# The rows of the MLP turned by VectorE and a scratch in device memory instead of by TensorE

## What is computed

```python
h = _ln(win, ln1_g, ln1_b)
q, k, v = h @ wq + bq, h @ wk + bk, h @ wv + bv
attn = softmax(q k^T / sqrt(32));  o = attn @ v
win = win + (o @ wo + bo)
h2 = _ln(win, ln2_g, ln2_b)
win = win + gelu(h2 @ w1 + b1) @ w2 + b2        # w1: 96 x 384, w2: 384 x 96
```

## Time and profile before

| | |
|---|---|
| median of 3 runs | 5434.65 us (5433.81 to 5440.99) |
| the profiled execution | 5443.81 us, span 5442.0 us |
| PE busy | 5176.5 us, 95% of the span |
| DVE / ACT / POOL busy | 77% / 69% / 57% |
| DMA queue of SyncE | 208 MB, 13.0% of 16 engines' span |

### The profile page before, as it was taken

One profiled execution on the slowest core, in us unless ns is written; L12 is line 12 of the kernel. 1 busy time (PEld: TensorE's weight loads), 2 busy tenths in 40 slices (PEclk: granted clock), 3 DMA queues, 4 the chain that ended last, 5 costly groups with the idle time before them and its releaser, 6 DMA issues.

```text
span 5442.0 us, 275140 instructions
## 1 busy us (share of the span) xinstructions
PE 5176.5 (95%) x105172; PEld 4395.4 (81%) x105172; DVE 4179.8 (77%) x9862; ACT 3741.6 (69%) x7758; POOL 3083.7 (57%) x3053
## 2 busy tenths in 40 slices
PE   6999999999999999999999999999999999999999
PEld 4887888878788787888878888788887888878888
DVE  6968768687686877869778697786977869688696
ACT  6839568495784957749477594875938659396693
POOL 5645646466464655646556466464664646556464
PEclk8999999999999999999999999999999999999999
DMA  3011020110201102010120201202011020110201
GB/s 98 3 44 48 27 68 6 47 42 27 68 9 51 36 30 65 11 57 27 33 62 15 61 19 36 59 16 66 13 38 57 19 70 6 41 54 22 73 3 44
DMA packets 92300, 213.96 MB, mean 39 GB/s; under 512 B 22058, under 2 KB 26379, under 8 KB 91851
## 3 DMA queue, kind: packets, MB, share of 16 engines
q1 hardware_dynamic: 91848, 208.20, 13.0%
q10 hardware_dynamic: 2, 0.00, 0.0%
HBM read 107.45 MB, written 100.66 MB: 38 GB/s over the span
## 4 chain that ended last, share of the span: by engine, by line
PE 88%; issue 5%; DVE 5%; SPq 1%; ACT 1%; POOL 0%; DVEq 0%; ACTq 0%; DMA 0%; POOLq 0%
PE psum L585 20%; PE psum L599 19%; PE psum L462 12%; PE psum L430 8%; PE psum L508 6%; PE psum L477 6%; PE psum L494 6%; PE psum L538 5%; PE psum L524 5%; DVE row_max L828 1%; DVE stats L807 1%; DVE stream L857 1%; SPq L251 1%; DVE probs L835 0%; DVE prob_sum L843 0%
## 5 line engine op out<-in xcount | busy, mean ns | idle before, releaser
L297 POOL TENSOR_TENSOR probs<-probs,prob_inv 128x512 f32<-128x512 f32 x771 | 783.1, 1044 | 1496.7 <-DVE prob_inv L851 1496.6
L857 DVE TENSOR_TENSOR stream<-stream,psum 128x384 f32 x1024 | 562.4, 553 | 850.3 <-PE psum L599 760.8
L736 ACT ACTIVATE gelu_odd<-psum 128x512 f32<-128x512 f32 x768 | 459.9, 599 | 732.7 <-PE psum L585 676.9
L736 ACT ACTIVATE gelu_even<-psum 128x512 f32<-128x512 f32 x768 | 459.6, 598 | 682.8 <-PE psum L585 627.1
L376 POOL TENSOR_TENSOR stream<-stream,b_all 128x768 f32 x256 | 493.2, 1931 | 612.4 <-DVE normed L877 584.8
L659 ACT ACTIVATE normed<-stream,shift,rstd 128x96 f32 (+1 forms) x2072 | 770.7, 461 | 43.9 <-POOL shift L345 23.2
L807 DVE BATCH_NORM_STATS2 stats<-stream (+2 forms) x4224 | 725.9, 243 | 57.1 <-DVE stream L857 38.9
L336 POOL TENSOR_TENSOR rstd<-variance,minus_half 128x32 f32<-128x32 f32 (+3 forms) x181 | 747.7, 4131 | 14.2
L304 POOL TENSOR_TENSOR hT<-hT_upper,hT_lower 96x1024 f32<-96x1024 f32 x258 | 613.6, 2378 | 22.8 <-issue 15.6
L828 DVE TENSOR_REDUCE row_max<-psum 128x8 f32<-128x512 f32 x771 | 523.8, 679 | 131.7 <-PE psum L494 116.6
L843 DVE TENSOR_REDUCE prob_sum<-probs 128x8 f32<-128x512 f32 x771 | 497.8, 679 | 109.1 <-ACT probs L693 109.1
(11 more groups left out here) (86 smaller groups left out, 10635.3 us busy)
## 6 DMA issues: line engine op xcount, KB each, us to landing
stream<-in_x SPq DMA_DIRECT2D x272, 192.0 KB
out<-stream SPq DMA_DIRECT2D x256, 192.0 KB
stream<-in_x SPq DMA_DIRECT2D x272, 180.0 KB
out<-stream SPq DMA_DIRECT2D x256, 180.0 KB
stream<-in_x SPq DMA_DIRECT2D x544, 6.0 KB
out<-stream SPq DMA_DIRECT2D x512, 6.0 KB
gelu_odd<-in_L_conv_w SPq DMA_DIRECT2D x1, 144.0 KB
w_w<-in_L_conv_w SPq DMA_DIRECT2D x1, 144.0 KB
```

The lines of the kernel that those rows point to most:

```text
L297: nc.gpsimd.tensor_tensor(block_h, block_h, inv, ALU.mult).then_inc(probs_ready, 1)
L736: nc.scalar.activation(gelu[parity][:, j, part * SHARES:(part + 1) * SHARES], psum[:, UP_BANKS[part][j], :], ACT.Gelu).then_inc(gelu_done, 1)
L857: nc.vector.tensor_tensor(part, part, psum[:, banks[g], 0:GROUP], ALU.add).then_inc(added, 1)
```

## The change

The 8 transposes of each MLP unit leave TensorE. VectorE turns the normalised rows in blocks of 32x32 (`turn_h2`), which puts 32 channels of a tile on the 32 partitions of each block. SyncE sends the turned rows to a scratch in device memory with 3 DMAs, one for each block of 32 channels (`send_turned`), waits until they are there, and fetches them back as 96 partitions by 1,024 numbers with one DMA (`fetch_turned`). The scratch has 4 places; the fetched units alternate between two buffers, those of `probsT` and `oT` in the MLP stage. ScalarE makes the upper half (`copy_h2T_upper`, two copies of 96x512), VectorE the first half of the lower, GpSimd the second. Tokens arrive in another order, which `gelus` puts right by the pattern it writes with.

Units 0, 1 and 2 of a batch are normalised by GpSimd, turned by VectorE and sent during the attention stage; units 0 and 1 are also fetched there, and GpSimd makes both their halves at steps 11 and 13. `down` now waits for both parts of the Gelu and comes in one piece. The diff, cut:

```diff
+        turned_dram = nc.dram_tensor("turned_rows", (RING, CBLOCKS, BLOCK, TBLOCKS, RUN), FP32, kind="Internal").ap()
+        turned_early = gelu[1][:, 2, 0:SEG]
+        turned_late = flat_tile(normed1[:, :, :])
+        raw_early = [gelu[0][0:C, 0, :], gelu[0][0:C, 1, :]]
+        raw_late = [probsT[0:C, :, :, :].rearrange("c h q k -> c (h q k)")[:, 0:TOK], oT[0:C, :]]
...
+            def send_turned(u, source, place):
+                wait_apart(sp, h2_turned, u + 1)
+                for cb in range(CBLOCKS):
+                    sp.dma_start(turned_dram[place, cb].rearrange("c t x -> t c x"),
+                                 source[:, RUN * cb:RUN * (cb + 1)]).then_inc(h2_left, 16)
+            def fetch_turned(u, raw, place):
+                wait_apart(sp, h2_left, 16 * CBLOCKS * (u + 1))
+                sp.dma_start(raw, turned_dram[place].rearrange("b c t x -> (b c) (t x)"))\
+                    .then_inc(h2_back[place % 2], 16)
+            def fetch_late(u, place):
+                for ready in h2T_ready:
+                    wait_apart(sp, ready, u - 1)
+                fetch_turned(u, raw_late[place % 2], place)
             def store_batch(batch_row):
-                with sp.Fori(0, BATCH_ROWS) as r:
+                batch = 2 * batch_row
+                for n in range(2):
+                    send_turned(batch + n, turned_early, n)
+                    fetch_turned(batch + n, raw_early[n], n)
+                send_turned(batch + 2, turned_early, 2)
+                wait_apart(sp, pv_done, batch + BATCH)
+                fetch_turned(batch + 2, raw_late[0], 2)
+                send_turned(batch + 3, turned_late, 3)
+                fetch_late(batch + 3, 3)
+                with sp.Fori(0, 3) as q:
+                    for n in range(RING):
+                        store(batch_row + 2 * q + n // 2, n % 2)
+                        send_turned(batch + 4 * q + n + 4, turned_late, n)
+                        fetch_late(batch + 4 * q + n + 4, n)
+                for row in (6, 7):
                     for half in (0, 1):
-                        store(batch_row + r, half)
+                        store(batch_row + row, half)
...
+            def copy_h2T_early(u, parity):
+                wait_apart(pool, h2_back[parity], 8 * (u - parity) + 16)
+                whole, upper, lower = raw_early[parity], h2T[parity][0][0:C, :], h2T[parity][1][0:C, :]
+                nc.gpsimd.tensor_copy(upper, whole).then_inc(h2T_upper_early, 1)
+                return whole, upper, lower
+            def lower_early(b, u, parity, parts):
+                whole, upper, lower = parts
+                pool.wait_ge(h2T_upper_early, 2 * b + parity + 1)
+                nc.gpsimd.tensor_tensor(lower, whole, upper, ALU.subtract).then_inc(h2T_ready[0], 1)
+                pool.sem_inc(h2T_ready[1], 1)
+            def copy_h2T_lower(b, j, u, parity):
+                second = slice(SHARES, 2 * SHARES)
+                wait_apart(pool, h2T_upper_done, 2 * (BATCH - 2) * b + 2 * (j - 2) + 2)
+                nc.gpsimd.tensor_tensor(h2T[parity][1][0:C, second], raw_late[parity][:, second],
+                                        h2T[parity][0][0:C, second], ALU.subtract).then_inc(h2T_ready[1], 1)
...
                     if s == 3:
                         finish2(call, batch, 0, 2)
+                    if s == 4:
+                        normalise2(b, batch, 0)
                     if s == 5:
-                        finish2(call + 1, batch + 2, 2, 2)
+                        finish1(call + 1, batch + BATCH, 0, 2)
+                    if s == 6:
+                        normalise2(b, batch + 1, 1)
                     if s == 7:
-                        normalise2(b)
+                        finish1(call + 2, batch + BATCH + 2, 2, 1)
+                    if s == 8:
+                        finish2(call + 3, batch + 2, 2, 2)
+                    if s == 9:
+                        normalise2(b, batch + 2, 2)
                     if s == 10:
-                        finish1(call + 2, batch + BATCH, 0, 2)
+                        finish2(call + 4, batch + 4, 4, 2)
+                    if s == 11:
+                        lower_early(b, batch, 0, copy_h2T_early(batch, 0))
                     if s == 12:
-                        finish1(call + 3, batch + BATCH + 2, 2, 1)
+                        finish2(call + 5, batch + 6, 6, 2)
+                    if s == 13:
+                        lower_early(b, batch + 1, 1, copy_h2T_early(batch + 1, 1))
                     normalise_probs(batch + s + 1, (s + 1) % 2)
                 for j in range(BATCH):
+                    if j < BATCH - 2:
+                        copy_h2T_lower(b, j + 2, batch + j + 2, j % 2)
...
-            def transpose2(u, steady):
-                pe.wait_ge(ln2_ready, u + 1)
+            def up(u, parity, part, steady):
+                pe.wait_ge(h2T_ready[part], u + 1)
                 if steady:
-                    pe.wait_ge(gelu_done, 2 * FCHUNKS * u - FCHUNKS)
-                for g in range(2):
-                    transpose_rows(normed2, T2_BANKS, g, t2_done)
-            def up(u, parity, part, steady):
-                pe.wait_ge(h2T_copied, 2 * u + 1 + part)
-                if part and steady:
-                    pe.wait_ge(gelu_done, 2 * FCHUNKS * u)
+                    wait_apart(pe, gelu_done, 2 * FCHUNKS * u - FCHUNKS * (1 - part))
...
+            def mlp_step(u, parity):
+                up(u, parity, 1, True)
+                up(u + 1, 1 - parity, 0, True)
+                down(u, parity, True)
...
+                    in_rows = gelu[parity][:, j, :].rearrange("p (t b i) -> p b t i", b=TBLOCKS, i=BLOCK)
+                    nc.scalar.activation(
+                        in_rows[:, 2 * part:2 * part + 2, :, :],
+                        psum[:, UP_BANKS[part][j], :].rearrange("p (b t i) -> p b t i", b=2, i=BLOCK),
+                        ACT.Gelu).then_inc(gelu_done, 1)
+            def copy_h2T_upper(u, parity):
+                act.wait_ge(h2_back[parity], 8 * (u - parity) + 16)
+                for g in range(2):
+                    tokens = slice(g * SHARES, (g + 1) * SHARES)
+                    nc.scalar.activation(h2T[parity][0][0:C, tokens], raw_late[parity][:, tokens], ACT.Copy)\
+                        .then_inc(h2T_upper_done, 1)
...
+                gelus(batch, 0, 0)
+                with act.Fori(0, BATCH // 2 - 1) as k:
+                    for odd in (0, 1):
+                        j = 2 * k + odd
+                        gelus(batch + j, odd, 1)
+                        copy_h2T_upper(batch + j + 2, odd)
+                        gelus(batch + j + 1, 1 - odd, 0)
...
-            def copy_h2T(u, parity):
-                upper, lower = h2T[parity]
-                tokens = [slice(g * SHARES, (g + 1) * SHARES) for g in range(2)]
-                for g in range(2):
-                    dve.wait_ge(t2_done, 2 * u + g + 1)
-                    nc.vector.tensor_copy(upper[0:C, tokens[g]], psum[0:C, T2_BANKS[g], :])\
-                        .then_inc(upper_step, 1)
-                for g in range(2):
-                    dve.wait_ge(upper_step, 2 * u + g + 1)
-                    nc.vector.tensor_tensor(lower[0:C, tokens[g]], psum[0:C, T2_BANKS[g], :],
-                                            upper[0:C, tokens[g]], ALU.subtract).then_inc(h2T_copied, 1)
+            def turn_h2(u, turned, first):
+                dve.wait_ge(ln2_ready, u + 1)
+                if not first:
+                    wait_apart(dve, h2_left, 16 * CBLOCKS * u)
+                nc.vector.transpose(turned.rearrange("p (b t i) -> p t b i", b=CBLOCKS, i=BLOCK),
+                                    normed2[:, :, :].rearrange("p t (b i) -> p t b i", i=BLOCK))\
+                    .then_inc(h2_turned, 1)
+            def copy_h2T_lower(b, j, parity):
+                first = slice(0, SHARES)
+                dve.wait_ge(h2T_upper_done, 2 * (BATCH - 2) * b + 2 * (j - 2) + 1)
+                nc.vector.tensor_tensor(h2T[parity][1][0:C, first], raw_late[parity][:, first],
+                                        h2T[parity][0][0:C, first], ALU.subtract).then_inc(h2T_ready[0], 1)
...
+                whole_step(5)
+                turn_h2(batch, turned_early, True)
+                whole_step(6)
+                whole_step(7)
+                whole_step(8)
+                turn_h2(batch + 1, turned_early, False)
+                whole_step(9)
+                whole_step(10)
+                whole_step(11)
+                turn_h2(batch + 2, turned_early, False)
...
-                    copy_h2T(batch + j + 1, 1 - parity)
-                    normalise2(batch + j + 2, j + 2)
-                    if row is not None:
-                        statistics1(batch + BATCH + AHEAD + j, AHEAD + j, batch_row + BATCH_ROWS + row, half)
-                    scale2(b, j + 2)
+                    normalise2(batch + j + 3, j + 3)
+                    scale2(b, batch + j + 3, j + 3)
```

(84 more changed lines are left out.)

75 lines of the change are left out of this document (35 added, 40 removed).

## The result

The changed kernel takes **5650.22 us** (median of 4 runs, 5644.51 to 5651.98) where the kernel before takes 5437.03 (median of 4, 5433.81 to 5440.99): ratio 1.0387, interval 1.037 to 1.0403. It is 213 us slower. The forecast was 5490, so 53 us slower. The sign held. The range of 5200 to 5660 held too, near its upper end. The size did not: the loss is four times the forecast one.

A forecast was written before the change was run, and what follows sets the result against it. PE bound the kernel; after the change SP's 10.3 us round would. Per batch, 2.1 us more in the MLP stage and 1.4 in attention, times 16, made 56 on 5443.8: 5500 profiled, 5490 forecast, range 5200 to 5660.

The forecast's parts named there:

- rival A: MLP stage: SP's round with sends on 4 engines sets the pace, 10.3 us a round, 5490 us; chance 0.53.
- case C: MLP stage: send at the crowded rate, 5.7 us of data, round 11.6, program 5740 us; chance 0.15.
- SP free for the rounds: MLP stage start: first send done and fetch issued 11.5 us after the last output projection ends.
- twelve rounds: SP's queue, units 4 to 15: store, send, wait for landing and fetch, 10.3 us each.
- last fetch until ACT copies: End of MLP stage: 1.3 us to first data and some 1.2 of data until unit 15 is back.
- from there to the end: End of MLP stage: 3.2 us of ACT's copy and Gelus, then 12.5 us of PE's remaining matmuls.
- the send: SP's round: 1.3 us to first data, 4.5 of data on 4 engines, 0.1 for the semaphore, 5.9 us.
- The attention stage: Three block transposes added on DVE, half counted on the path: 1.4 us more per batch.
- Block transpose: DVE's turn of a unit's rows, taken as 0.94 us like the nearest pass; upper bound 3 us.
- hidden under PE: MLP stage: added DVE, ACT and POOL work fits under PE's 8.41 us per unit; DVE at most 8.0.
- T1: Experiments' theory: SyncE's round, long through sends on 4 engines, sets the pace; for e1 it gave 5180 to 5250 us.
- rival B: MLP stage: sends spread over 16 engines, round 7.7 us, PE keeps the pace at 8.41, 5203 us; chance 0.27.

The follow-up runs named there:

- e1: The changed kernel with each send cut by blocks of 32 partitions into 4 DMAs on 16 engines instead of 3 on 4: 5385.93 us.
- e2: The changed kernel with each send cut by rows into 6 DMAs of outermost count 2, so on 2 engines: 6614.77 us.
- e4: The changed kernel with sends on 16 engines as in e1, and GpSimd adding b2 two units ahead: 5206.72 us.
- e5: The changed kernel, sends still on 4 engines, with only GpSimd's additions of b2 moved two units ahead: 5716.51 us.

## Why the prediction was half right

**What bound (right).** PE paced, and stopped pacing once the rows had to travel. The round on SyncE's queue became the bound in the MLP stage (rival A, the forecast). 4 engines per send, argued from the outermost count, was right, shown by 7,167 new final packets against 7,168, and by e1 and e2, which moved the time by writing the same bytes with other outermost counts. The other reading, 16 engines by the 128 partitions, falls. The rule of the Trainium skill (DMA: Bandwidth & Descriptors, "Why a DMA increments its semaphore by 16 and not by 1"), that the count on *both* sides matters, agrees with all of this. The runs do not show it whole: the counts in device memory (2, 4, 32) were never the larger ones (in SBUF 64, 128, 32), so a rule by that side alone would fit as well. The same page's fit ("Anatomy of one DMA — SWDGE (gpsimd) path"), 2.0 us plus bytes over 436 GB/s, is given for a DMA that GpSimd issues, while these are issued by SyncE; by it a send's 393 KB would take 2.9 us, an estimate. Measured are 6.6 on 4 engines and 3.5 on 16, and the measurement decides.

**How near the sign was.** By the forecast's own sum a round of 10.0 us would have left the time unchanged, and its round was 10.3. With the lower bound of the data time, 3.9 us, the same sum gave 5375, a gain. So the sign rested on a choice inside bounds of 1.8 us. Case A's own range ended at 5620, below the 5650 measured, and case C's 5740 lay outside the range of 5200 to 5660 that was said to take in most of it: that the range held is in part luck.

**The size (wrong).** The sum for a batch was z + 152.6; it became z + 163.86. Its terms:

| term | forecast | measured | more |
|---|---|---|---|
| SP free for the rounds | z + 11.5 | z + 13.9 | 2.4 |
| twelve rounds | 123.6 | 129.9 | 6.3 |
| last fetch issued before the round's end | 0.7 | 1.1 | -0.4 |
| last fetch until ACT copies | 2.5 | 3.2 | 0.7 |
| from there to the end | 15.7 | 17.9 | 2.2 |

- *Rounds.* The failed term is the send, 5.9 forecast and 6.6 measured. (Of the signs named ahead these did show: ACT's waits for `oT` and `probsT`, PE's busy share of 89% in the stage, 4 final packets a send, a DMA share of a quarter. Units were to be 10.3 us apart and are 10.8. Two did not: the stage was to last about 152 us and lasts 164, and PE was to idle once per unit and waits for a Gelu 117 times in 256 units, mostly for the odd one, whose rows come behind the longer store.) Its data were put at 4.5 us, between 3.9 and 5.7, and took 5.0 in the send looked at above; the step behind them was put at 0.1 and took 0.35. The other parts of a round came out at 4.2 against 4.4. So 0.7 us more on the send, about 0.5 on the round, 6.3 over twelve of them. The text had said what that is worth: 19 us of time for each 0.1.
- *Start.* Three things lie in the 2.4 us: the first send was issued at z + 6.3 instead of z + 4.9 (idle steps between VectorE's instructions, such as the 0.62 and 0.24 in the brackets of the rows above, were left out of the sum), the send took 6.5 instead of 5.9, and from the fetch's issue to the first store 1.06 us passed instead of 0.7.
- *Tail.* PE's last two units were counted at full clock. PE had waited, and the granted clock of the stage fell to 0.94, in the window 2732 to 2736 to 0.60. At the half level (1.2 GHz) a matmul of 128x512 takes 0.63 us, not 0.39:

```profile
2732.45 0.63 PE L656 MATMUL psum<-h2T_odd_upper,w_split_lower 128*128 128x512 f32 x1
```

```profile
2840.39 0.47 PE L656 MATMUL psum<-h2T_odd_upper,w_split_upper 128*128 128x512 f32 x1 [2.58 <-ACT gelu_even L805]
2844.00 4.35 PE L671 MATMUL psum<-w_w,gelu_even 128*64 128x96 f32 x96
```

  The last up half but one takes 3.6 us (2840.39 to 2844.00) instead of 2.1. Another 0.76 us is a wait of the last down projection for ACT's Gelu, which the sum left out; it stands in e4 too:

```profile
2851.41 4.18 PE L671 MATMUL psum<-w_w,gelu_odd 128*64 128x96 f32 x96 [0.76 <-ACT gelu_odd L805]
```

  From the fifth unit of the stage on PE waits about every second unit and runs slower matmuls behind the wait. In all it is busy for 145.98 us in the stage, where e4 needs 134.70 for as many matmuls at a clock of 1.00. While SyncE's round sets the pace, this slowness does not lengthen the stage; behind the last fetch it does, and no term of the forecast had it.

The terms add to 11.2 us a batch, 180 in all. The attention stage went the other way: forecast +1.4, measured about -1.0 for the mean of two batches, so 2.4 x 16 = 38 less. 5500 + 180 - 38 = 5642 in the frame of the profiled execution, which took 5648.95. Why attention did not grow was not tried.

**Block transpose (right).** 0.98 us, forecast 0.94, mean of 208 0.979.

**VectorE and GpSimd "hidden under PE" (half wrong).** In the changed kernel they are hidden, but under SyncE's round. Under PE they would not have been: e1 came 136 us above T1's upper end, and the prediction's rival B had nothing of that. Its 5203 was the time of another order of work on GpSimd (e4), and with the send on 16 engines alone the kernel would have taken 5386. The cost was looked for in GpSimd's busy time (88 of 150 us), and it lay in its order. Also, VectorE's and GpSimd's durations were taken as fixed. The first of the two normalising passes took 945 ns on average before and takes 1,866 now; the second hardly changed (964 and 1,002). That a pass stretches beside GpSimd's additions is shown at the start of e5's stage; that this is all of the 1,866 is not shown.

```profile
L954 DVE TENSOR_TENSOR normed<-stream,mean 128x768 f32 x192 | 358.2, 1866 | 27.7 <-issue 20.2
```

**Left open.** The early split of units 0 and 1 on GpSimd was not undone by itself; its share of the result, a gain at the start of the stage or a loss in attention, is not known. Whether the rows could be turned without device memory, or the stores moved to another queue, was not tried.

## What to carry to other kernels

Before rows are sent through a transfer that something waits for, write out the queue's round (issues, data, landing) and count the DMA engines by the outermost counts of the transfer (here the one in device memory, the smaller, decided); the same bytes with another order of dimensions took 3.5 us instead of 6.6 and turned a loss of 4% into a gain of 1%. Then ask what comes next: an engine with time to spare can still be late, if a small step that others wait for stands behind a long one in its queue, and that shows only when the first bound is gone (another 3%). A fix for the second bound is worth nothing while the first stands; here it even cost 1%.

## What the runs showed of the hardware

- VectorE's fp32 pass over 128x768 takes 0.96 us while GpSimd is idle (the changed kernel, 2694.70) and 2.39 and 2.64 us in e5 beside GpSimd's fp32 additions on SBUF. The block transpose keeps 0.98 there, beside a subtraction on GpSimd.
- GpSimd's power on 128x32 takes 5.44 us in e1 (mean over the changed kernel 5.52).
- A send of 128x768 fp32 in 1 KB rows takes 11.3, 6.6 and 3.5 us until its fetch can be issued, on 2, 4 and 16 engines (k). The first two give 1.9 us + 18.8 us / k, an estimate by which 16 engines would take 3.1. The sends differ in their number of DMAs too (6, 3 and 4), so the 1.9 us are not shown to be fixed.
- Behind a wait of 2.20 us the granted clock was 0.60 over the next 4 us, so at the 1.2 GHz level for most of them, and the stage as a whole fell from 1.00 to 0.94.
